# A new cyclic order of the attention step on all engines, and TensorE's loop over layers unrolled

## The reference, cut to what matters

```
for i in range(6):                       # DEPTH, b = 2, n = 1024, 16 heads of 64
    qkv = shift_tokens(x) @ Wqkv[i]      # 128 -> 3 x 1024
    q, k = l2norm(q) * q_scale, l2norm(k) * k_scale
    q = q*cos*scale + rotate_half(q)*sin*scale      # k with 1/scale
    sim = 8 * q @ k.T                    # windows of 32 queries on 64 keys, masked
    out = softmax(sim) @ v
    x = out @ Wo[i] + x
    x = ffn(shift_tokens(x)) + x         # layernorm, 128 -> 2 x 341, gelu gate, -> 128
```

## Time and profile before

| | us |
|---|---|
| median of 3 runs | 2471.7 (2471.47 to 2472.44) |
| profiled execution | 2466.07 |
| its span | 2464.3 |
| PE busy, share of the span | 2083.0 (85%) |
| DVE busy | 1839.4 (75%) |
| ACT busy | 1536.3 (62%) |
| POOL busy | 1306.1 (53%) |

### The profile page before, as it was taken

One profiled execution on the slowest core, in us unless ns is written; L12 is line 12 of the kernel. 1 busy time (PEld: TensorE's weight loads), 2 busy tenths in 40 slices (PEclk: granted clock), 3 DMA queues, 4 the chain that ended last, 5 costly groups with the idle time before them and its releaser, 6 DMA issues. The chain is left out here.

```text
span 2464.3 us, 81247 instructions
## 1 busy us (share of the span) xinstructions
PE 2083.0 (85%) x33532; PEld 1457.6 (59%) x33532; DVE 1839.4 (75%) x3984; ACT 1536.3 (62%) x5170; POOL 1306.1 (53%) x869
## 2 busy tenths in 40 slices
PE   5649999799998999998999989999999982764287
PEld 2337667477574775756757567575775741433265
DVE  4569779498795886958969679596896947675744
ACT  2239778387694885957959579595885932551122
POOL 1138678277683785837858468584783811211000
PEclk8679999999999999999999999999999995876699
DMA  2011111111011110101101011011110100001000
GB/s 94 0 37 40 33 30 48 35 43 37 25 53 34 39 39 22 51 24 54 41 20 53 25 52 40 20 52 29 51 38 16 38 10 11 1 0 52 1 0 17
DMA packets 86567, 80.49 MB, mean 33 GB/s; under 512 B 15040, under 2 KB 82624, under 8 KB 85568
## 3 DMA queue, kind: packets, MB, share of 16 engines
q1 hardware_dynamic: 86208, 75.37, 10.6%
HBM read 25.51 MB, written 1.05 MB: 11 GB/s over the span
## 5 line engine op out<-in xcount | busy, mean ns | idle before, releaser
L988 POOL TENSOR_TENSOR RN<-N,minus_half 128x8 f32<-128x8 f32 x384 | 698.7, 1820 | 18.4 <-DVE N L940 18.4
L984 POOL TENSOR_TENSOR RR<-R 128x512 f32<-128x512 f32 x384 | 488.2, 1271 | 383.3 <-DVE R L933 383.3
L829 ACT ACTIVATE PB<-PS,NMX 128x64 f32<-128x64 f32 x1536 | 460.4, 312 | 69.1 <-DVE NMX L950 69.0
L708 PE MATMUL PS<-WQ,XS 128*128 128x256 f32 x1536 | 438.6, 408 | 13.4 <-SPq L539 13.1
L651 PE MATMUL PS<-ident,QK 128*128 128x128 f32 x1536 | 254.7, 289 | 68.0 <-issue 30.4
L829 ACT ACTIVATION_READ_ACCUMULATOR PB<-PS,NMX 128x1 f32 x1536 | 311.3, 203 | 0.0
L708 PEld LDWEIGHTS PS<-WQ,XS 128*128 128x128 f32 x1536 | 262.9, 191 | 69.7 <-SPq L539 13.4
L808 ACT ACTIVATE QKT<-PS 128x512 f32<-128x512 f32 x384 | 229.6, 598 | 63.0 <-PE PS L651 46.9
L940 DVE TENSOR_REDUCE N<-SQ 128x8 f32<-128x512 f32 x384 | 257.1, 670 | 11.3 <-ACT SQ L803 11.2
L919 DVE SCALAR_TENSOR_TENSOR QK<-RN,RR 128x512 f32<-128x512 f32 x384 | 262.5, 684 | 1.4 <-POOL RR L984 1.2
L932 DVE TENSOR_TENSOR R<-PS,COSL 128x512 f32<-128x512 f32 x384 | 260.0, 677 | 0.0
(11 more groups left out here) (208 smaller groups left out, 3399.3 us busy)
## 6 DMA issues: line engine op xcount, KB each, us to landing
VS<-XB SPq DMA_DIRECT2D x384, 96.0 KB, 2.1
VS<-XB SPq DMA_DIRECT2D x288, 32.0 KB, 2.1
WQ<-in_wqkv SPq DMA_DIRECT2D x40, 192.0 KB, 2.4
WO<-in_wo SPq DMA_DIRECT2D x6, 512.0 KB
BIG<-in_wgu SPq DMA_DIRECT2D x1, 2048.0 KB, 8.1
W<-in_w SPq DMA_DIRECT2D x6, 341.0 KB
WQ<-in_wqkv SPq DMA_DIRECT2D x1, 1536.0 KB, 11.3
QKS<-in_qks SPq DMA_DIRECT2D x6, 256.0 KB, 3.5
```

Of the source, the lines that this page charges most:

```text
L708: mm = nc.tensor.matmul(PQ[:, (g + 3) % 2, j * 256:(j + 1) * 256], XSb[b][:, t0:t0 + P], WQ[:, pair * 384:pair * 384 + 256], start=True, s ...
L829: ex = nc.scalar.activation(PB[:, g % 2, u, :], SC[:, h, DH * t:DH * t + DH], ACT.Exp, bias=NMX[:, u:u + 1], accum_out=PSUMS[:, g % 2, u:u ...
L984: nc.gpsimd.tensor_tensor(RR[:, :, :], R1[:, :, :], R2[:, :, :], ALU.add)\
L988: nc.gpsimd.tensor_tensor(RN[:, g % 2, :], N2[:, g % 2, :], minus_half[:, :], ALU.pow)
```

## The change

Each engine's `step(g)` gets a new order.

- PE: transposes QK(g); queries and keys (g+3), now behind a wait for `rot_in` (sine product of g+1 written) where POOL's `pq_free` was; wait for the copied values, tell SP; outputs, now of g-3; masks (g), behind `sc_free` in every step; probabilities' transposes (g-2) and values (g+1); scores (g); feed-forward, with waits that look ahead (`peek`) at the copied values and outputs.
- ACT: QKT (g); outputs' copy (g-3); squares, now of g+3; XB; exponentials (g).
- DVE: squares' sum (g+2); cosine, now of g+2, into R1 or its new second buffer R1B; normalisation, now of g-2; wait for RR(g+1); sine, now of g+2; product, now of g+1; reciprocal (g-1); maxima (g).
- POOL: the sum RR(g+1) also waits for the product of g (`qk_in`).

The flows `pq_free` and `p_in` go. PE's program has no loop: all 390 steps are straight, with one `settle()` at the end.

```diff
+        R1B = sb("R1B", [P, CB, 256])
...
+                        if there(g + 3):
+                            l, b, pair, c = where(g + 3)
+                            if g + 3 > 1:
+                                pe.wait_ge(rot_in.sem, g + 2)
...
+                            mm.then_inc(proj_in.sem, 1)
+                        if there(g) or there(g - 3):
+                            pe.wait_ge(vp_in.sem, vp_in.take())
+                        if there(g):
+                            pe.sem_inc(v_in.sem, 1)
+                        if there(g - 3):
+                            c = (g - 3) % CH
+                            if g - 3 > 0:
...
+                            mm.then_inc(o_ps.sem, 1)
                         if feed_forward_at(g - 1):
                             pe.wait_ge(ffn_pe.sem, ffn_pe.take())
+                        if there(g):
+                            c = g % CH
+                            if g > 0:
+                                pe.wait_ge(sc_free.sem, sc_free.take())
...
-                            masks_early = g > 0 and g + 2 < TOTAL
-                            if masks_early:
...
+                            pe.wait_ge(qkt_in.sem, qkt_in.take())
...
                         if ffn:
+                            if values or probs:
+                                pe.wait_ge(vp_in.sem, vp_in.peek(1))
+                            pe.wait_ge(o_free.sem, o_free.peek(1))
                             feed_forward(*ffn, g)
...
-                    LAYER = B * SLOT
-                    for g in range(-3, 3):
+                    for g in range(-3, TOTAL + 3):
                         step(g)
-                    settle()
-                    with pe.Fori(0, LAYERS - 1):
-                        for g in range(3, 3 + LAYER):
-                            step(g)
-                        settle()
-                    for g in range(3 + TOTAL - LAYER, TOTAL + 3):
-                        step(g)
-                    pe.wait_ge(pq_free.sem, pq_free.take(2))
+                    pe.wait_ge(sc_free.sem, sc_free.take())
+                    pe.wait_ge(o_free.sem, o_free.take())
                     pe.wait_ge(ffn_pe.sem, ffn_pe.take())
...
+                        if there(g + 3):
+                            act.wait_ge(proj_in.sem, proj_in.take())
+                            nc.scalar.activation(SQ[:, (g + 3) % 2, :, :].rearrange("p g d -> p (g d)"),
+                                                 PQ[:, (g + 3) % 2, :], ACT.Square).then_inc(sq_in.sem, 1)
+                        if values or probs:
+                            cols = slice(0 if values else 256, 512 if probs else 256)
+                            act.wait_ge(vp_ps.sem, vp_ps.take())
+                            nc.scalar.activation(XB[:, (g + 1) % CH, cols], PX[:, cols], ACT.Copy)\
+                                .then_inc(vp_in.sem, 1)
...
+                        if there(g + 2):
+                            l, b, pair, c = where(g + 2)
+                            t = slice(CB * c, CB * c + CB)
+                            qk = PQ[:, g % 2, :].rearrange("p (j n) -> p j n", j=CB)
+                            qk5 = qk.rearrange("p j (g v d) -> p j g v d", v=2, d=DH // 2)
+                            dve.wait_ge(sq_in.sem, sq_in.take())
+                            nc.vector.tensor_reduce(N2[:, g % 2, :], SQ[:, g % 2, :, :], AX.X, ALU.add)\
+                                .then_inc(n2_in.sem, 1)
...
+                            nc.vector.tensor_tensor(R1k[g % 2][:, :, :], qk, COSk[l % 2][:, t, :], ALU.mult)
+                        if there(g - 2):
+                            k = g % 2
+                            dve.wait_ge(ro_in.sem, ro_in.take())
+                            nc.vector.tensor_tensor(
+                                PB[:, k, :, :], PB[:, k, :, :],
+                                RO[:, k, :].unsqueeze(2).to_broadcast([P, 4, 2 * WIN]), ALU.mult)\
+                                .then_inc(pn_in.sem, 1)
+                        if there(g + 1):
+                            dve.wait_ge(rr_in.sem, rr_in.take())
+                        if there(g + 2):
                             nc.vector.tensor_tensor(
                                 R2s[:, :, :, :, :].rearrange("p j g v d -> p (j g) v d"),
                                 qk5[:, :, :, ::-1, :].rearrange("p j g v d -> p (j g) v d"),
                                 SINs[l % 2][:, t, :, :, :].rearrange("p j g v d -> p (j g) v d"), ALU.mult)\
                                 .then_inc(rot_in.sem, 1)
...
+                        if there(g + 1):
+                            k = (g + 1) % 2
+                            nc.vector.scalar_tensor_tensor(QKg[k], RN[:, k, :].unsqueeze(2)
+                                                           .to_broadcast([P, 8, DH]), 1e12, RRg,
+                                                           ALU.min, ALU.mult)\
+                                .then_inc(qk_in.sem, 1)
...
+                            dve.wait_ge(sc_free.sem, g)
                             nc.vector.reciprocal(RO[:, k, :], PSUMS[:, k, :]).then_inc(ro_in.sem, 1)
...
-                            pool.sem_inc(pq_free.sem, 1)
-                            nc.gpsimd.tensor_tensor(RR[:, :, :], R1[:, :, :], R2[:, :, :], ALU.add)\
+                            if g + 1 > 0:
+                                pool.wait_ge(qk_in.sem, g + 1)
+                            nc.gpsimd.tensor_tensor(RR[:, :, :], R1k[(g + 1) % 2][:, :, :], R2[:, :, :],
+                                                    ALU.add)\
```

More of the change, by code:

```diff
@@ L605, in gate_and_up @@
                             cols, w = slice(h * HALF, (h + 1) * HALF), FJ[j]
-                            if i == 0 and g + 3 < TOTAL:
+                            if i == 0 and there(g):
                                 pe.wait_ge(sc_free.sem, sc_free.peek(1))
@@ L653, in step @@
                             tr.then_inc(qkt_ps.sem, 1)
+                        if there(g + 3):
+                            l, b, pair, c = where(g + 3)
+                            if g + 3 > 1:
+                                pe.wait_ge(rot_in.sem, g + 2)
+                            if g + 3 > 0 and (g + 3) % SLOT == 0:
+                                pe.wait_ge(xs_in.sem, xs_in.take(4))
+                            if b == 0 and c == 0:
+                                pe.wait_ge(wq_in.sem, wq_in.take())
+                            for j in range(CB):
+                                t0 = (CB * c + j) * P
+                                mm = nc.tensor.matmul(PQ[:, (g + 3) % 2, j * 256:(j + 1) * 256],
+                                                      XSb[b][:, t0:t0 + P],
+                                                      WQ[:, pair * 384:pair * 384 + 256],
+                                                      start=True, stop=True)
+                            mm.then_inc(proj_in.sem, 1)
@@ new lines, in step @@
+                        if there(g) or there(g - 3):
[6 more added lines that the diff above has]
+                                pe.wait_ge(o_free.sem, o_free.take())
+                            for w in range(4):
+                                for t in range(2):
+                                    for h in range(2):
+                                        keys = slice(2 * WIN * t, 2 * WIN * t + 2 * WIN)
+                                        vals = VX if w % 2 else VS
+                                        cols = 256 + P * h + WIN * w
+                                        mm = nc.tensor.matmul(
+                                            PO[DH * h:DH * h + DH, t, WIN * w:WIN * w + WIN],
+                                            vals[keys, c, w // 2, DH * h:DH * h + DH],
+                                            XB[keys, g % CH, cols:cols + WIN],
+                                            start=True, stop=True)
+                            mm.then_inc(o_ps.sem, 1)
@@ L654, in step @@
                         if feed_forward_at(g - 1):
                             pe.wait_ge(ffn_pe.sem, ffn_pe.take())
+                        if there(g):
+                            c = g % CH
+                            if g > 0:
+                                pe.wait_ge(sc_free.sem, sc_free.take())
+                            for h in range(2):
+                                nc.tensor.matmul(
+                                    SC[:, h, 0:P], identb[:, :],
+                                    bandmask[:, 0 if c == 0 else 1, :, :].rearrange("p t k -> p (t k)"),
+                                    start=True, stop=False)
@@ L697, in step @@
                             mm.then_inc(sc_in.sem, 1)
[L698 to L712, removed]
```

80 lines of the change are left out of this document (8 added, 72 removed).

## The result

The changed kernel takes 2409.1 us (median of 4 runs, 2405.99 to 2414.87), the kernel before 2471.6 on the same chip: a ratio of 0.9736, 95% interval 0.971 to 0.9762, 62.5 us less. The profiled execution took 2405.99 us, its span 2404.1. Against the profiled 2466.07 of before it is 60 us less, where 84 were forecast. The time is inside the range and 21 us above the predicted 2388.

A forecast was written before the change was run, and what follows sets the result against it. A chain through VectorE and TensorE, the product behind the normalisation, was taken to bound the 3.54 us step. Ordinary steps 58, plus unrolling 40, minus SyncE 14, gave 84 us: 2388, range 2355 to 2432.

The forecast's parts named there:

- rival A: On VectorE the normalisation stays long, so the step is 3.51 us and the kernel 2425 us; chance 0.20.
- signs named for a right forecast: Step 3.35 to 3.42, normalisation 0.41 and power 1.64, no 7 us idle at layer ends, TensorE waiting 15 or 20 on SyncE.
- SyncE's queue: SyncE's moves of values and weight loads fall behind a shorter step, making TensorE wait: 14 us lost, bounds 5 and 25.
- the second new loop: Two-step chain from product through TensorE, scores, maxima and VectorE to the next but one product: 6.77 us, half 3.38.
- TensorE's sum: TensorE's own work per step in the new order, added up without waits: 3.36 us.
- the first loop: One-step chain: normalisation, its transposes, values, scores, maxima, squares' sum, cosine product, next normalisation: 3.34 us.
- The normalisation's overlap: GpSimd's power now begins inside VectorE's cosine product, 0.2 us ahead of the normalisation, which takes 0.41; other bound 0.59.
- rival C: Power beginning inside the cosine product lengthens it, and the normalisation stays long: step 3.68, kernel slower at 2483 us; chance 0.06.
- TensorE unrolled: Straight code without TensorE's loop over layers removes the cost of its jumps: 40 us gained, bounds 34 and 44.
- Rival B: Unrolling TensorE gives nothing, as straight code runs short of instructions once a layer: 2428 us; chance 0.06.
- Feed-forward steps: Steps around the feed-forwards stay as they were but for their one ordinary step: 0 us, bounds -4 and +4.
- D: Rival: TensorE's terms were too long, the step falls to 3.28, SyncE takes 25 back: 2363 us; chance 0.12.

## Why the prediction was right, and what it had wrong

The measured 2409 lies inside the range, but nearer to rival A's 2425 than to the forecast 2388, so the time alone would not tell them apart; the rows do. Of the signs named for a right forecast two hold (normalisation 0.41 with the power near 1.64, no idle time of 7 us at the ends of layers) and two don't (a step of 3.35 to 3.42, waits for SyncE's queue of 15 or 20).

- *Which loop bounds the step.* The three candidates were the right ones, the choice among them was not: the forecast took the second new loop, 3.38, and it is the first, 3.46, put at 3.34. The second was well forecast. It sets the step where the values are taken out of the first (6.77 for two steps, forecast 6.77), a hair above TensorE's sum of 3.37 (forecast 3.36), and where the normalisation is moved forward and gets longer (7.00).
- *Size of the first loop: the failed term.* "0.41+0.05" for the normalisation and its pick-up was 0.56. The 0.05 came from the product's pick-up, which TensorE waits for with one wait. The normalisation stands behind the second of two waits, and its transposes start 0.15 behind its end (1003.97+0.41 to 1004.53). Exchanging the two brings it to 0.06 and the step to 3.40. The transposes and values were 0.79 instead of 0.76; with no wait ahead of them, in the kernel with the normalisation moved, they take 0.77, so most of that belongs to the wait as well. The step gained 0.08 instead of 0.16: over 361 steps 28 us instead of 58. That is more than the whole difference between forecast and result.
- *The normalisation's overlap.* Right: 0.41, the power 1.65, the cosine product 0.68 with the power beginning in it (rival C's condition, without its price). Rival A's mechanism is real, as the exchange on VectorE shows at 0.68 and 1.83, but the new order keeps out of it. The rule of the Trainium skill ("GPSIMD Engine Reference", Key points) holds there; by it the normalisation in the changed kernel should be longer too, as it lies wholly beside the power, and it isn't.
- *TensorE unrolled.* 40 with bounds of 34 and 44; an estimated 35 once the share of the clock and of SyncE is taken off. The jump from which the prediction read 11.3 us (753.73 to 813.48) has one of the two feed-forwards with long matmuls in it, 1.7 us that are not the jump's. Rival B's loss isn't there: the stalls of 1.7 us in the unrolled kernels are the clock, not a shortage of instructions.
- *Feed-forward steps.* Within the bounds. Three steps over one, as in the prediction's 48.47, are 48.28 (584.51 to 632.79 by the products). Of the 0.19 between them 0.08 is the ordinary step's, so the order's own share is 1 us in all.
- *SyncE's queue.* The mechanism is right, the size followed the step: 14 more were charged for 3.38, and TensorE's waits are 5.6 us at 3.46, 2 more than before. They cost more than they last. Behind two of them (1.2 us at 1033, 1.5 at 1620) TensorE's clock stood at 0.50 for over 3 us. The steps held up are 10 us longer than undisturbed ones, 4 in the kernel before: 6 more, inside the bounds of 5 and 25. At a step of 3.40 the row has 12.4, with values first 10.9, and with the weights' wait moved it is gone.
- *The sum.* Ordinary steps 28, unrolling 35, feed-forwards 1, less 6 for SyncE: 58, where the products show 61.6 and the profiled executions 60. Of the other 4, 1.7 is one feed-forward fewer with long up and gate matmuls; the rest lies in small stalls of the kernel before. So 30 us were missing in the ordinary steps and 5 in the unrolling, and 8 came back since SyncE's queue had a slower step to keep up with: that the result came as near as 21 us is in part this offset. Rival A's time of 2425 and D's of 2363 were both missed.

## What to carry to other kernels

When a step is bound by a closed loop over two engines, every hand-over in it counts once a step: put the wait that ends last first where two stand ahead of one instruction, and keep work that doesn't belong to the loop (here the values) ahead of that wait, not behind it. A term for a hand-over is to be read from one with the same number of waits. Where several loops lie within a few per cent, add them all up again after each change: here the next one took over 0.08 below the first. When the order of a tight step is changed, look again at the queue that was just fast enough, and at what TensorE's clock does in the stretches with waits, since both can take back the gain elsewhere.

## What was not expected of the hardware

- Where two waits stood ahead of the probabilities' transposes, the second cost TensorE 0.15 us from the release to the start, the first 0.06. The second is a sequencer instruction of 51 ns that runs from 0.04 to 0.09 behind the release; what fills the time up to 0.15 wasn't tested. One place of the program showed it.
- TensorE's clock fell to its lower level (0.59 granted over a stretch of 3.2 us) in single feed-forwards, right behind two waits of 0.33 and 0.87 us, while the same waits in other feed-forwards of the same execution left it whole. The same kernel had it in the up and gate matmuls of one of eleven in one profile and of seven in another, so a difference of some us between two profiles can be this alone. With the longer wait filled with work none of the eleven had it, in the one profile there is. What decides between the cases stays open.
- GpSimd's power and VectorE's normalisation lengthen each other (0.41 to 0.68, 1.65 to 1.83) when the power begins inside the normalisation, not when the normalisation begins and ends inside the power. One pair of instructions showed it; others weren't tried.
